# Local attention products of the scan: eight 128x128 block diagonal products in place of 32 of 32x32

## The chip, the cores and the metric

The kernel runs on one core of one Trainium2 chip. The core has a matrix engine (TensorE, in the profile PE for products and PEld for weight loads), VectorE (DVE), ScalarE (ACT), GpSimd (POOL) and SyncE (SP), which issues the DMAs. The metric is the device time of one execution in microseconds.

## What is computed

Two transformer blocks over x of shape (16, 512, 128). The change lies in the second block's attention, a scan over 16 segments of 32 positions, with 16 heads of width 64:

```python
def step(carry, inp):
    mem, z = carry
    q_s, k_s, v_s, qn_s, kn_s = inp
    scores = jnp.einsum('bhnd,bhmd->bhnm', q_s, k_s) * SCALE
    scores = jnp.where(mask, scores, -jnp.inf)
    sdpa = jnp.einsum('bhnm,bhmd->bhnd', jax.nn.softmax(scores, axis=-1), v_s)
    sq = elu1(qn_s)
    num = jnp.einsum('bhnk,bhkv->bhnv', sq, mem)
    den = jnp.einsum('bhnk,bhk->bhn', sq, z)[..., None]
    mem_out = num / (den + 1e-06)
    out = beta * mem_out + (1.0 - beta) * sdpa
    sk = elu1(kn_s)
    prev_v = jnp.einsum('bhnk,bhkv->bhnv', sk, mem) / jnp.einsum('bhnk,bhk->bhn', sk, z)[..., None]
    mem = mem + jnp.einsum('bhnk,bhnv->bhkv', sk, v_s - prev_v)
    z = z + sk.sum(axis=2)
    return ((mem, z), out)
```

The local product is `sdpa`: for each batch and head a 32x32 matrix of exponentials of scores times the 32x64 values; the division by the sums follows in the next stage.

## The kernel before

The program runs stage after stage: weights folded, the first block's projections (`front`), its attention (`attend`), the closing of both (`tail`), routing and experts, and from about 1.68 ms on the scan (`scale_factors`, then `scan`).

The scan handles a pair of heads at a time: 16 segments times 8 pairs are 128 pairs. The 16 batches lie as BG = 4 groups g in the free dimension and B1 = 4 f in the partitions: partitions 32f to 32f+31 hold the 32 positions of batch 4g + f. A tile of a pair therefore has eight "channels" ch = 2g + hh (group and head of the pair) in the free dimension and four f in the partitions.

The order is written by hand: each engine has a loop over steps s, unrolled, and in step s each handles several pairs at different stages. In step s TensorE (the loop at the end of `turn`) does, in this order: query projection of pair s (L2037); local product of pair s-2 (L2071); values of pair s (L2043); key recall of s-2 (L2053 with `sk`); transposes of keys (L2089), mask (L2077) and scores (L2082) of s-1; key projection of s (L2037); query recall of s-2 (L2053 with `sq`); output projection of s-4 (L2101); transpose of heads of s-3 (L2094); memory update of s-4 (L2061). At some steps of each eight, work for the next segment is added (L1883, L1889, L2106, L2176).

VectorE in step s: L2268 scales the local product of s-2 out of PSUM bank 6; rope of the query of s (L2240, L2241) and its feature (L2247); L2278 and L2280 for the key recall; L2285 and L2286 on the scores of s-1; L2297, L2298 and L2300 for the query recall; rope of the key (L2240, L2241); then for pair s-1 the 32x32 transposes of the exponentials `ss` into `pT` (L2306), their sums (L2308) and the reciprocal (L2309); then the memory additions (L2257). Rounding and moments for the next segment stand at some steps between L2286 and L2297 or before.

ScalarE in step s: query features of s (L2186, L2191); copies of the turned keys (L2200) and of the values (L2204); the exponential of the scores of s-1 (L2208); key features (L2186, L2188, L2191); the copy of turned heads (L2220); and at some steps normalization for the next segment (L1863, L1869) and copies of its turned input (L1895, L1899).

Engines wait on named counters (`G[...]`). The local product of pair p waits until `pt` has reached p + 1, and `pt` rises with the reciprocal L2309, so after transpose and sums. The transposed exponentials are the stationary operand, the values the moving one. An f32 product stands in the trace as two weight loads and two matmul records.

Of the kernel before, what the change touches and what calls it, by code (L numbers as in the profile page):

```python
# [25 lines left out]
P = 128  # L26
# [1584 lines left out]
B1, SEG, DH = 4, 32, 64  # L1611
# [3 lines left out]
PAIRS = H // 2  # L1615
# [149 lines left out]
def scan(nc, c, V, out, nseg):  # L1765
# [4 lines left out]
    with ExitStack() as ctx:  # L1770
        sb = lambda n, s, d=F32: ctx.enter_context(nc.sbuf_tensor("sc_" + n, s, d))
        sems = []

        def sem(n):
# [8 lines left out]
        uu = V["uu"]  # L1783
# [8 lines left out]
        GH = 2 * BG  # L1792
        ss, pT = sb("ss", [P, 2, GH, SEG]), sb("pT", [P, 4, GH, SEG])
        mx, sm = sb("mx", [P, GH]), sb("sm", [P, 4, GH])
        rk, rq = sb("rk", [P, GH]), sb("rq", [P, GH])
# [5 lines left out]
        names = ("h_in0 h_in1 stat fact shift_d xn_d tq_d xnn_d xq_d step xt xt_c xqt xqt_c hb_d ffn ffn_c vp v_c pj ex mn rp sn sgq sgk add_d sS skt skc "  # L1801
                 "sx se pt pvd old kr_s qr_s kd ud qd od up mu ott otc oproj yt_c yt ydone stored0 stored1").split()
        G = {n: sem(n) for n in names}
# [3 lines left out]
        def wait(eng, name, n):  # L1807

            if n > 0:
                eng.wait_ge(G[name], n)  # L1810
# [5 lines left out]
        def linker(eng):  # L1816
            count = [0]

            def link(ins):

                count[0] += 1
                ins.then_inc(G["step"], 1)
                eng.wait_ge(G["step"], count[0])
            return link
# [76 lines left out]
        def prepare(seg):  # L1901

            with nc.Block() as block:
# [5 lines left out]
                @block.vector  # L1909
                def _(dve):  # L1910
                    link = linker(dve)
                    moments(dve, link, 0)
                    shifts(dve, 1)
                    round_fp8(dve, link, 1)
# [24 lines left out]
        def turn(seg, more):  # L1939
# [33 lines left out]
            with nc.Block() as block:  # L1973
# [58 lines left out]
                def _(pe):  # L2032
# [33 lines left out]
                    def local(p):  # L2066
                        for g in range(BG):
                            for hh in range(2):
                                for f in range(B1):
                                    ch = 2 * g + hh  # L2070
                                    ins = pe.matmul(ps[32 * f:32 * f + 32, 6, ch * DH:(ch + 1) * DH], pT[32 * f:32 * f + 32, p % 4, ch, :],  # L2071
                                                    uu[32 * f:32 * f + 32, p % PAIRS, g, hh, 0:DH], start=True, stop=True)
                        ins.then_inc(G["pvd"], 1)
# [35 lines left out]
                    for s in range(STEPS):  # L2109
# [5 lines left out]
                        if inside(p):  # L2115
                            wait(pe, "otc", min(s - 3, PT))
                            wait(pe, "pt", p + 1)
                            local(p)
# [61 lines left out]
                def _(act):  # L2180
                    def features(n):
# [9 lines left out]
                        act.activation(ee[:, which], ee[:, which], ACT.Exp, scale=-1.0).then_inc(G["mn"], 1)  # L2191

                    for s in range(STEPS):
                        if s < PT:
                            features(2 * s)
# [36 lines left out]
                def _(dve):  # L2232
# [26 lines left out]
                    for s in range(STEPS):  # L2259
                        p = s - 2  # L2260
                        if inside(p):
                            wait(dve, "pvd", p + 1)
                            wait(dve, "pt", p + 1)
                            wait(dve, "ott", p - 3)
# [39 lines left out]
                        if inside(p):  # L2304
                            wait(dve, "se", p + 1)
                            dve.transpose(pT[:, p % 4].rearrange("p c j -> p (c j)"), ss[:, p % 2].rearrange("p c j -> p (c j)"))  # L2306
                            s_ = sm[:, p % 4]
                            link(dve.tensor_reduce(head(s_), by_head(ss[:, p % 2]), AX.X, ALU.add))  # L2308
                            dve.reciprocal(s_, s_).then_inc(G["pt"], 1)  # L2309
                        if s - 7 in starts:  # L2310
# [155 lines left out]
```

## Time and profile before

| | us |
|---|---|
| median of 3 runs | 3109.3 |
| lowest, highest | 3105.91, 3112.54 |
| profiled execution | 3109.39 |
| span of its trace | 3107.6 |
| TensorE busy, products | 2664.5 (86%) |
| VectorE busy | 2506.4 (81%) |
| ScalarE busy | 1875.9 (60%) |
| GpSimd busy | 1758.7 (57%) |

Busy times are shares of the whole span, and stages differ. A row of a timeline gives the start and the length of a group of equal instructions in us, the engine and the line, what is written and read, the shape and the count; in brackets how long the engine was idle before it and what ended that. "Issue" is idle time in which the engine waited for nothing that the profile shows. Rows of a matmul overlap: the time from one row's start to the next one's is what a stage costs, not its length. The granted clock (PEclk) is 1.00 at 2.4 GHz and 0.50 at 1.2 GHz.

### The profile page before, as it was taken

The numbers are of one execution on the slowest core, as the hardware profiler recorded it, in microseconds if no ns is written. First come the engines' busy times: TensorE is split into PE (matmuls) and PEld (weight loads), VectorE is DVE, ScalarE is ACT, GpSimd is POOL, SyncE is SP. The second block draws the span as 40 slices with busy tenths as digits, with TensorE's granted clock in tenths as the row PEclk, the third lists the DMA queues.
The fourth block names the chain that finished last, engine by engine and source line by source line (L and its number), as shares of the span: only waits on it lengthen the run. The fifth ranks groups of instructions, "written<-read, shape, count | busy, mean of one in ns | idle before, by whom it ended". The sixth has DMA issues, their size and how long they took to land. (4 is left out here: it accounts for less than half of the span.)

```text
span 3107.6 us, 129631 instructions
## 1 busy us (share of the span) xinstructions
PE 2664.5 (86%) x53553; PEld 1513.6 (49%) x53553; DVE 2506.4 (81%) x7598; ACT 1875.9 (60%) x3797; POOL 1758.7 (57%) x1988
## 2 busy tenths in 40 slices
PE   5887999999999999782331899999999998999998
PEld 2442333333333333372220666666666666666665
DVE  4677989999999999586606888888888888888887
ACT  5785999999999999630001555555455555555543
POOL 5883222222222222240063888888888888888886
PEclk9896999999999999895655999999999999999999
DMA  4676434444444443191023000000000000000000
GB/s 126 205 241 155 90 89 94 94 107 94 91 94 98 96 94 87 39 325 55 10 40 91 4 11 11 11 11 4 11 11 11 11 11 11 11 11 5 11 8 11
DMA packets 173633, 201.58 MB, mean 65 GB/s; under 512 B 31152, under 2 KB 134512, under 8 KB 172784
## 3 DMA queue, kind: packets, MB, share of 16 engines
q1 hardware_dynamic: 170480, 191.87, 23.8%
q8 instruction: 427, 7.00, 1.0%
q0 software_dynamic: 2560, 1.35, 0.4%
q14 instruction: 166, 1.36, 0.2%
HBM read 125.10 MB, written 67.24 MB: 62 GB/s over the span
## 5 line engine op out<-in xcount | busy, mean ns | idle before, releaser
L851 ACT ACTIVATE at_pA<-at_ps 128x512 f32<-128x512 f32 x1024 | 551.8, 614 | 57.8 <-DVE at_ps L903 51.1
L912 DVE CUSTOM_DVE_ANT_0 at_junk<-at_ps,w_cmask 128x512 f32<-128x512 f32 (+3 forms) x1024 | 463.4, 485 | 102.7 <-PE at_ps L754 95.4
L903 DVE TENSOR_TENSOR at_ps<-at_ps,w_ratio 128x128 f32<-128x128 f32 (+3 forms) x1024 | 451.2, 491 | 2.1 <-PE at_ps L748 0.5
L720 POOL TENSOR_SCALAR_AFFINE_SELECT at_pB<-at_pB 128x128 f32<-128x128 f32 x256 | 74.8, 292 | 640.4 <-ACT at_pB L857 638.3
L857 ACT ACTIVATE at_pB<-at_ps 128x512 f32<-128x512 f32 (+1 forms) x768 | 379.5, 531 | 53.0 <-PE at_ps L761 47.7
L2001 POOL TENSOR_TENSOR sc_rb<-sc_rb,v_sin 128x512 f32<-128x512 f32 x256 | 326.0, 1274 | 42.4 <-DVE sc_ra L2241 41.1
L2037 PE MATMUL sc_ps<-sc_xT,v_wqkv 128*128 128x512 f32 x512 | 287.2, 644 | 4.0 <-PEq L56 1.4
L748 PE MATMUL at_ps<-at_aq,at_ak 72*128 72x512 bf16 x1024 | 278.3, 388 | 0.2
L2200 ACT COPY sc_skN<-sc_ps 128x512 f32<-128x512 f32 x128 | 75.1, 587 | 324.8 <-PE sc_ps L2089 324.8
L1996 POOL TENSOR_TENSOR sc_sk<-sc_ee,sc_relu 128x512 f32<-128x512 f32 x128 | 165.4, 1293 | 180.8 <-ACT sc_ee L2191 180.7
L761 PE MATMUL at_ps<-at_bq,at_bk 75*128 75x512 bf16 (+3 forms) x1024 | 265.8, 302 | 1.5 <-ACT at_pB L857 0.9
L781 PE MATMUL at_ps<-at_pA,at_v 128*32 128x512 f32 x2048 | 263.0, 609 | 1.2 <-ACT at_oT L840 1.2
L754 PE MATMUL at_ps<-at_bk,at_bq 72*128 72x512 bf16 (+3 forms) x1024 | 225.3, 306 | 20.3 <-PEq L56 11.7
L2186 ACT ACTIVATE sc_ee<-sc_ps 128x512 f32<-128x512 f32 x256 | 150.4, 587 | 110.9 <-PE sc_ps L2037 109.9
L2240 DVE STREAM_SHUFFLE sc_rb<-sc_ps 128x512 f32<-128x512 f32 x256 | 189.4, 740 | 0.0
L2071 PEld LDWEIGHTS sc_ps<-v_uu,sc_pT 32*32 32x32 f32 x8192 | 126.7, 106 | 118.7 <-issue 112.1
L2241 DVE TENSOR_TENSOR sc_ra<-sc_ps,v_cos 128x512 f32<-128x512 f32 x256 | 172.1, 672 | 0.0
L2004 POOL TENSOR_TENSOR sc_kr<-sc_ra,sc_rb 128x512 f32<-128x512 f32 x128 | 163.0, 1273 | 10.0
L2004 POOL TENSOR_TENSOR sc_qr<-sc_ra,sc_rb 128x512 f32<-128x512 f32 x128 | 162.5, 1270 | 10.0
L2257 DVE TENSOR_TENSOR v_mem<-v_mem,sc_ps 128x520 f32<-128x520 f32 x256 | 161.8, 674 | 6.0 <-PE sc_ps L2061 6.0
L2191 ACT ACTIVATE sc_ee<-sc_ee 128x512 f32<-128x512 f32 x256 | 161.4, 631 | 8.2
L2029 POOL TENSOR_TENSOR sc_ol<-sc_ol,sc_t 128x512 f32<-128x512 f32 x128 | 163.1, 1274 | 5.1 <-DVE sc_t L2300 5.1
(317 smaller groups left out, 5949.9 us busy)
## 6 DMA issues: line engine op xcount, KB each, us to landing
parts_scratch<-fr_parts SPq DMA_DIRECT2D x64, 384.0 KB, 4.1
at_bk<-parts_scratch SPq DMA_DIRECT2D x192, 96.0 KB
at_ak<-parts_scratch SPq DMA_DIRECT2D x192, 96.0 KB
v_scratch<-fr_v SPq DMA_DIRECT2D x32, 352.0 KB, 4.4
at_v<-v_scratch SPq DMA_DIRECT2D x32, 352.0 KB, 3.5
at_bq<-parts_scratch SPq DMA_DIRECT2D x128, 64.0 KB
at_aq<-parts_scratch SPq DMA_DIRECT2D x128, 64.0 KB
on_scratch<-at_on SPq DMA_DIRECT2D x32, 256.0 KB, 2.2
```

Of the source, the lines that this page charges most:

```text
L748: pe.matmul(ps[:, BANK[f"A{j}"], :], ak[slot][:, n % 4, j * P:(j + 1) * P], aq[slot][:, n % 4], start=True, stop=True).then_inc(filled, 1)
L754: ins = pe.matmul(ps[:, BANK[kind], col:col + wide], bq[slot][0:ROWS, n % 4, j * P:(j + 1) * P], bk[slot][0:ROWS, n % 4, 0:wide], start=Tr ...
L761: ins = pe.matmul(ps[:, BANK[kind], col:col + S - j * P], bk[slot][:, n % 4, j * P:(j + 1) * P], bq[slot][:, n % 4, j * P:S], start=True, ...
L781: ins = pe.matmul(ps[32 * s:32 * s + 32, PV, q0:S], v[:, b % 2, a, j, h * (HD + 1):h * (HD + 1) + 32], probs, start=(j == 0), stop=(j == N ...
L851: act.activation(pA[:, n % A_RING, j * S:(j + 1) * S], src, ACT.Exp).then_inc(exped, 1)
L857: act.activation(pB[:, n % T_RING, at:at + wide], src[:, 0:wide], ACT.Exp).then_inc(exped, 1)
L903: dve.tensor_tensor(src[:, 0:wide], src[:, 0:wide], W["ratio"][:, S - wide:S], ALU.mult).then_inc(tilted, 1)
L912: ins = dve.tensor_tensor_reduce(junk[:, P * j * (j + 1) // 2:P * (j + 1) * (j + 2) // 2], src[:, col:col + wide], W["cmask"][:, S - wide: ...
L2001: pool.tensor_tensor(by_pos(rb[:, n % 2]), by_pos(rb[:, n % 2]), table("sin", which), ALU.mult).then_inc(G["sn"], 1)
L2004: pool.tensor_tensor(rot[which][:, p % 2], ra[:, n % 2], rb[:, n % 2], ALU.add).then_inc(G["add_d"], 1)
L2037: pe.matmul(ps[:, bank_of("qk"[which], p), :], V["wqkv"][:, col:col + P], xT[:, p // PAIRS % 2], start=True, stop=True).then_inc(G["pj"], 1)
L2240: dve.stream_shuffle(rb[:, n % 2], x, [lane ^ 1 for lane in range(32)])
```

## The change

The local product of a group and a head is made as one 128x128 product. Its stationary operand is a block diagonal matrix: block f of channel ch stands in rows 32f and columns 32f of a new buffer `pB`, which has two sides and is zeroed once before the scan. ScalarE copies the blocks from `pT` into it with four copies (one per f, each 32 partitions, eight channels, 32 columns), at the head of its step. TensorE waits for the new counter `pb` in place of `otc` and `pt`. `pt` now rises with the transpose; VectorE's L2268 waits for the new counter `smd`, which rises with the reciprocal.

```diff
+        pB = sb("pB", [P, 2, GH, B1, SEG])
...
                     link = linker(dve)
+                    dve.memset(pB[:], 0.0)
                     moments(dve, link, 0)
...
                     def local(p):
                         for g in range(BG):
                             for hh in range(2):
-                                for f in range(B1):
-                                    ch = 2 * g + hh
-                                    ins = pe.matmul(ps[32 * f:32 * f + 32, 6, ch * DH:(ch + 1) * DH], pT[32 * f:32 * f + 32, p % 4, ch, :],
-                                                    uu[32 * f:32 * f + 32, p % PAIRS, g, hh, 0:DH], start=True, stop=True)
+                                ch = 2 * g + hh
+                                ins = pe.matmul(ps[:, 6, ch * DH:(ch + 1) * DH], pB[:, p % 2, ch].rearrange("p f j -> p (f j)"),
+                                                uu[:, p % PAIRS, g, hh, 0:DH], start=True, stop=True)
                         ins.then_inc(G["pvd"], 1)
...
                         if inside(p):
-                            wait(pe, "otc", min(s - 3, PT))
-                            wait(pe, "pt", p + 1)
+                            wait(pe, "pb", p + 1)
                             local(p)
...
+                    def place_blocks(p):
+                        wait(act, "pt", p + 1)
+                        wait(act, "pvd", p - 1)
+                        for f in range(B1):
+                            ins = act.copy(pB[32 * f:32 * f + 32, p % 2, :, f], pT[32 * f:32 * f + 32, p % 4])
+                        ins.then_inc(G["pb"], 1)
+
                     for s in range(STEPS):
+                        p = s - 2
+                        if inside(p):
+                            place_blocks(p)
                         if s < PT:
                             features(2 * s)
...
                         if inside(p):
                             wait(dve, "pvd", p + 1)
-                            wait(dve, "pt", p + 1)
+                            wait(dve, "smd", p + 1)
...
                             wait(dve, "se", p + 1)
-                            dve.transpose(pT[:, p % 4].rearrange("p c j -> p (c j)"), ss[:, p % 2].rearrange("p c j -> p (c j)"))
+                            wait(dve, "pb", p - 3)
+                            dve.transpose(pT[:, p % 4].rearrange("p c j -> p (c j)"), ss[:, p % 2].rearrange("p c j -> p (c j)")).then_inc(G["pt"], 1)
                             s_ = sm[:, p % 4]
                             link(dve.tensor_reduce(head(s_), by_head(ss[:, p % 2]), AX.X, ALU.add))
-                            dve.reciprocal(s_, s_).then_inc(G["pt"], 1)
+                            dve.reciprocal(s_, s_).then_inc(G["smd"], 1)
```

ScalarE's queue at the end of one step and the head of the next, in the step that normalizes for the next segment. Before:

```order
L2220 COPY sc_oT<-sc_ps 128x512
L1863 ACTIVATE sc_xn<-sc_ht,sc_shift,sc_sc 128x128 x4
L1869 ACTIVATE sc_tq<-sc_xn,v_qs 128x512
L2186 ACTIVATE sc_ee<-sc_ps 128x512
L2191 ACTIVATE sc_ee<-sc_ee 128x512
L2200 COPY sc_skN<-sc_ps 128x512
```

And after, with the lines of the changed file:

```order
L2230 COPY sc_oT<-sc_ps 128x512
L1864 ACTIVATE sc_xn<-sc_ht,sc_shift,sc_sc 128x128 x4
L1870 ACTIVATE sc_tq<-sc_xn,v_qs 128x512
L2197 COPY sc_pB<-sc_pT 32x8x32 x4
L2186 ACTIVATE sc_ee<-sc_ps 128x512
L2191 ACTIVATE sc_ee<-sc_ee 128x512
L2210 COPY sc_skN<-sc_ps 128x512
```

The four copies stand between the next segment's normalization and the query features.

TensorE's queue around the local product. Before:

```order
L2101 MATMUL sc_ps<-sc_oT,v_wout 128x512
L2094 MATMUL sc_ps<-v_ident,sc_ol 128x128 x4
L2061 MATMUL sc_ps<-v_uu,sc_skN 64x65 x32
L2037 MATMUL sc_ps<-sc_xT,v_wqkv 128x512
L2071 MATMUL sc_ps<-v_uu,sc_pT 32x64 x32
L2043 MATMUL sc_ps<-v_wqkv,sc_xT 128x128 x4
```

And after:

```order
L2102 MATMUL sc_ps<-sc_oT,v_wout 128x512
L2095 MATMUL sc_ps<-v_ident,sc_ol 128x128 x4
L2063 MATMUL sc_ps<-v_uu,sc_skN 64x65 x32
L2039 MATMUL sc_ps<-sc_xT,v_wqkv 128x512
L2072 MATMUL sc_ps<-v_uu,sc_pB 128x64 x8
L2045 MATMUL sc_ps<-v_wqkv,sc_xT 128x128 x4
```

The place is the same; 32 products have become eight.

## Rows read from the trace of the kernel before

**Rows 1.** Busy time and count by engine, clock, DMA; scan's steady part.

```profile
core 0: us, PE busy (x) PEld busy (x) DVE busy (x) ACT busy (x) POOL busy (x), PEclk, DMA share, GB/s
1725.33:3078.69 1353.36, 1253.85 (x43176) 871.27 (x43177) 1160.96 (x2866) 694.34 (x1303) 1127.92 (x905) 0.99 0.04 10
```

**Rows 2.** The line of the local product: durations in ns, first and last start.

```profile
L2071 PE MATMUL sc_ps<-v_uu,sc_pT x8192: 211/214/312, 1714.4 to 3091.0; 32*32 32x64 f32 x200
```

**Rows 3.** Timeline of TensorE's products, one step.

```profile
2506.45 1.10 PE L2071 MATMUL sc_ps<-v_uu,sc_pT 32*32 32x64 f32 x64
2507.49 1.16 PE L2043 MATMUL sc_ps<-v_wqkv,sc_xT 128*128 128x128 f32 x8
...
2512.70 1.12 PE L2101 MATMUL sc_ps<-sc_oT,v_wout 128*128 128x512 f32 x2
2513.66 0.60 PE L2094 MATMUL sc_ps<-v_ident,sc_ol 128*128 128x128 f32 x4
...
2516.20 1.10 PE L2071 MATMUL sc_ps<-v_uu,sc_pT 32*32 32x64 f32 x64
```

**Rows 4.** Timeline of VectorE in the same step.

```profile
2511.53 0.42 DVE L2286 TENSOR_TENSOR sc_ss<-sc_ps,sc_mx 128x256 f32<-128x256 f32 x1
2512.81 0.17 DVE L2297 SCALAR_TENSOR_TENSOR sc_rq<-sc_ps,v_ibeta 128x8 f32<-128x8 f32 x1 [0.86 <-PE sc_ps L2053]
...
2515.09 0.43 DVE L2306 STREAM_TRANSPOSE sc_pT<-sc_ss 128x256 f32<-128x256 f32 x1
...
2515.85 0.20 DVE L2309 RECIPROCAL sc_sm<-sc_sm 128x8 f32<-128x8 f32 x1
```

**Rows 5.** Waits of TensorE in the steady part: us in total, times, longest.

```profile
PE sc_ps L2053 <- issue: 36.9, 62, 1.2
PE sc_ps L2082 <- issue: 19.4, 31, 1.5
PE sc_ps L2061 <- DVE sc_t L2300: 18.5, 19, 3.1
PE sc_ps L2071 <- DVE sc_sm L2309: 6.2, 11, 2.0
```

**Rows 6.** DMA queue of instructions in the steady part: packets, MB, share.

```profile
q8 instruction: 341, 5.59, 1.8%
```

**Rows 7.** Timeline of weight loads and products at L1028, before the scan.

```profile
1336.50 0.97 PEld L1028 LDWEIGHTS tl_ps<-w_wr,tl_xfT 128*128 128x128 f32 x8
1337.39 0.19 PEld L1005 LDWEIGHTS tl_ps<-w_woA,tl_onT 128*128 128x128 f32 x1
...
1336.61 0.96 PE L1028 MATMUL tl_ps<-w_wr,tl_xfT 128*128 128x8 f32 x8
```

**Rows 8.** Timeline of ScalarE in the step of rows 3 and 4.

```profile
2511.99 0.42 ACT L2208 ACTIVATE sc_ss<-sc_ss 128x256 f32<-128x256 f32 x1 [0.85 <-DVE sc_ss L2286]
2512.31 0.58 ACT L2186 ACTIVATE sc_ee<-sc_ps 128x512 f32<-128x512 f32 x1
...
2514.89 1.65 ACT L1863 ACTIVATE sc_xn<-sc_ht,sc_shift,sc_sc 128x128 f32<-128x128 f32 x4
2516.57 0.72 ACT L1869 ACTIVATE sc_tq<-sc_xn,v_qs 128x512 f32<-128x512 f32 x1
```

**Rows 9.** Timelines of two other steps with work for the next segment.

```profile
2347.61 1.65 ACT L1863 ACTIVATE sc_xnn<-sc_ht,sc_shift,sc_sc 128x128 f32<-128x128 f32 x4
...
2347.90 0.44 DVE L2306 STREAM_TRANSPOSE sc_pT<-sc_ss 128x256 f32<-128x256 f32 x1
...
2800.20 0.43 DVE L2306 STREAM_TRANSPOSE sc_pT<-sc_ss 128x256 f32<-128x256 f32 x1
...
2800.65 0.78 ACT L1895 ACTIVATE sc_xT<-sc_ps,v_b,v_g 128x512 f32<-128x512 f32 x1 [1.06 <-PE sc_ps L1883]
```

**Rows 10.** Busy time by engine and clock after a wait of 3.1 us.

```profile
2360.10:2366.00 5.90, 5.88 (x135) 4.09 (x135) 3.20 (x7) 2.00 (x3) 3.77 (x3) 0.50 0.01 3
```

**Rows 11.** Timeline of VectorE where the scan begins.

```profile
1684.33 0.87 DVE L1840 BATCH_NORM_STATS2 sc_st<-sc_ht 128x6 f32<-128x128 f32 x4 [4.41 <-DMA sc_ht<-h_scratch]
```

More of the change, by code:

```diff
@@ L1801, in scan @@
         names = ("h_in0 h_in1 stat fact shift_d xn_d tq_d xnn_d xq_d step xt xt_c xqt xqt_c hb_d ffn ffn_c vp v_c pj ex mn rp sn sgq sgk add_d sS skt skc "
-                 "sx se pt pvd old kr_s qr_s kd ud qd od up mu ott otc oproj yt_c yt ydone stored0 stored1").split()
+                 "sx se pt smd pb pvd old kr_s qr_s kd ud qd od up mu ott otc oproj yt_c yt ydone stored0 stored1").split()
         G = {n: sem(n) for n in names}
```

## Prediction

> **What bounds the kernel now.** The change touches the scan, the last 1.4 ms. I read first the busy time by engine over its steady part [rows 1]: TensorE 1253.85 of 1353.36 us, VectorE 1160.96, ScalarE 694.34, at a granted clock of 0.99. TensorE paces it, VectorE is close behind, ScalarE has room on average. The 8192 records of the local product [rows 2] are 64 for each of 128 pairs (an f32 product stands as two records), from 1714.4 to 3091.0; with about 1.0 us for the last product, that is (3090.1 - 1714.4) / 127 = 10.83 us for one step.
>
> Then one step in order of time. On TensorE [rows 3] the local product starts at 2506.45, the next stage at 2507.49, the query recall is over when L2101 starts at 2512.70, and the next local product starts at 2516.20: a clean step is 9.75 us, so 1.08 us a step is lost on average. On VectorE [rows 4] the chain that starts with the end of the query recall reads: 2512.70 recall over, 2512.81 L2297, 2515.09 transpose (over at 2515.52), 2515.85 the reciprocal L2309 (over at 2516.05), and 0.15 us later the local product starts. So there are two paths from 2512.70 to the next local product, TensorE's own work and VectorE's chain, and they end together: the chain has no slack. That is the place on which all that follows rests.
>
> What is lost besides [rows 5]: "issue" waits of TensorE, 71.3 us over ten rows of that view (the two largest, 36.9 and 19.4, stand in the recalls and the scores, stages of many small records), and waits for VectorE, 18.5 + 6.2. The issue waits look like instruction loading: 341 packets of 16 KB [rows 6] in 1353.36 us are one each 3.97 us, one for 253 of the 86353 records of [rows 1].
>
> **Local product on TensorE.** Removed: 64 records, 2506.45 to 2507.49, 1.04 us [rows 3]. Added: 8 f32 products of 128x128, 16 records, each with a load of 128 columns and only 64 columns to stream. The trace has that shape nearly: L1028 loads 128x128 f32 and streams 8 columns, and its eight loads take 1336.50 to 1337.39, 0.111 us each [rows 7]. With next to nothing to stream this is the price of the load. So 16 x 0.111 = 1.78 us, 0.74 more than before. By columns alone it would be less: L2101's two records of 512 columns take 2512.70 to 2513.66, 0.48 each [rows 3], so 64 columns 0.06 and the product 0.96. I take 1.78, since L1028 is the same load.
>
> The Trainium skill ("TensorE: Matmul & The Clock Gate", LDWEIGHTS) has a load cost its columns over 1.2 GHz whatever the rows. An estimate by that page is 107 ns a load and 1.71 us for the product; L1028's 0.111 agrees.
>
> **Placing on ScalarE.** Four copies 32x256, SBUF to SBUF, stand at the head of ScalarE's step and wait for the transpose; TensorE waits for the last of them. Nearest row: L2208, 128x256 f32 in SBUF, 0.42 us, and the next instruction starts 0.32 after it [rows 8]. 0.04 from VectorE (2511.53 + 0.42 to 2511.99), 3 x 0.32, 0.42: 1.42 us. A quarter of the partitions saves nothing in that reading, as lanes work side by side. Bounds: 0.2 a copy if fewer lanes were cheaper, 0.41 as the four 128x128 of L1863 show (1.65 / 4), which also read a scale and a shift. To TensorE another 0.15 as now, and 0.08 more for the first load, most of the 0.11 from load to product at L1028 (1336.50 to 1336.61).
>
> Moving the signal from the reciprocal to the transpose gives back 2516.05 - 2515.52 = 0.53, which the sum has, as it starts from the transpose. Behind the waiting copies on ScalarE stand the query features (L2186, L2191), which VectorE's next rope waits for; but VectorE stands at the local product itself then (L2268), and the features are over long before that product. So nothing is added there.
>
> **One clean step.** 1.78 (local) + 5.21 (2507.49 to 2512.70) + 0.11 + 2.71 (2512.81 to 2515.52) + 1.42 + 0.23 = 11.46 us, against 9.75. TensorE waits 1.0 us at each local product.
>
> **What comes on top, each step.**
> - ScalarE late: once in eight steps it has L1863 and L1869 for the next segment, until 2517.29, 1.77 after the transpose [rows 8]; a step later another four L1863 until 2349.26 against 2348.34, 0.92; then L1895 until 2801.43 against 2800.63, 0.80 [rows 9]; then a copy of the same kind, some 0.5 (no row, between 0.3 and 0.6). All this stands ahead of the copies and is hidden today. 3.99 / 8 = 0.50.
> - VectorE late (moments and rounding between the scores and L2297): 24.7 us of waits now [rows 5], 0.19 a step; 0.25, as no slack remains beside it.
> - Issue waits inside the part that still counts (all but 2512.70 to 2516.20): 36.9 + 19.4 among them, 0.45 a step. 48 products and 48 loads fewer of some 690 records, and a longer step, let loading keep up better; I take 0.25, bounds 0 and 0.45.
> - Clock: after the longest wait, 3.1 us [rows 5], the granted clock was 0.50 (1.2 GHz instead of 2.4) through 5.90 us [rows 10]. TensorE will now stand 1 us each step and 1.8 to 2.8 us in three of eight. 0.2 a step, bounds 0.1 and 0.5.
>
> Sum 12.66 us, 1.83 more than 10.83; times 127 = 232 us. The zeroing of the block buffer (128x2048 f32 on VectorE) falls into 4.41 us in which VectorE waits for the first load [rows 11]: nothing; at most some 3 us without it. Profiled execution 3109.4 us (span 3107.6), the median of the runs 3109.3; so 3341, I say 3340. With the low ends of all terms (place 1.06, late 0.4 and 0.15, issue 0, clock 0.1) a step is 11.75, 3226; with the high ones (place 1.69, late 0.6 and 0.35, issue 0.45, clock 0.5) 13.63, 3465. All at one end is unlikely: 3240 to 3425.
>
> **Rivals.**
> - Instruction loading decides (faster). If one packet each 3.97 us were a fixed rate and the true bound, a step of some 595 records instead of 691 takes 2.35 packets, 9.3 us, and TensorE's own work 9.75 + 0.74 = 10.49 ends last: 0.34 less, 3066. For it: 71.3 us of issue waits. Against: it holds only if the copies are over before TensorE arrives, thus if the added 0.96 of the chain falls under zero, and [rows 4] shows a chain without slack. 0.04.
> - Placing mostly hidden, TensorE alone pays: 0.74 - 0.25 = 0.49 a step, 3171. It needs copies of about 0.1 us each and ScalarE in time. 0.06.
> - Streaming, not loading, sets the product: 0.96 instead of 1.78, 104 us less than forecast, 3236. L1028 speaks against it, but it streams 8 columns, not 64. 0.06.
> - The clock falls more often: a stretch as that of [rows 10], 5.90 us at half speed, loses some 2.9 us, and with two of them in eight steps (after the two longest waits) the clock costs 0.73 a step, 0.53 beyond my 0.2, 3408. Against: the 3.1 us before it is one of 30 waits for VectorE, and most of those changed nothing. 0.14.
> - The forecast: 0.70.
>
> To the third belongs a sentence of the Trainium skill ("Perfetto Trace Analysis", Matmuls), that larger matmuls are more efficient than smaller ones. By that rule the eight large products should take less than the 1.04 us of the 32, some 0.96; the loads of L1028 speak against it here.
>
> **How the numbers follow.** A measurement of this kernel tells 0.2%, 6 us, from no change. Faster is the first rival, 0.04; within 0.2% is left 0.02 for mixtures of it with the second; slower 0.94. The range 3235 to 3425 holds the forecast and the third and the fourth rival.
>
> **What would show it.** Right: the eight products take 1.7 to 1.9 us with a load each 0.111; ScalarE's four copies take 1.4 us directly after the transpose; TensorE's wait at the local product names ScalarE and is about 1.0 us, some 2.7 in the step with L1863 and L1869; issue waits fall under 45 us; the clock has more low stretches. Wrong: no wait at the local product (placing hidden), 16 records within 1.1 us, copies that take a quarter of L2208's time, or a clock at 0.50 in a large part of the scan.

## The result and the profile after

| | before | after |
|---|---|---|
| median, us | 3109.24 | 3386.35 |
| lowest, highest | 3105.91, 3112.54 | 3374.75, 3388.92 |
| runs | 4 | 4 |
| span of the profiled execution | 3107.6 | 3387.2 |

The ratio of after to before is 1.0883, with a 95% interval of 1.0864 to 1.0902: the change costs 277 us, where the forecast said 231. The time is inside the range of 3235 to 3425.

The page after, the span, the busy shares, the granted clock in 40 slices, and the head of the chain that ended last:

```profile
span 3387.2 us, 117980 instructions
PE 2835.5 (84%) x47409; PEld 1700.3 (50%) x47409; DVE 2501.2 (74%) x7599; ACT 2076.1 (61%) x4309; POOL 1759.0 (52%) x1988
...
PEclk9887999999999998756579998999989999999999
...
PE 30%; DVE 8%; ACT 7%; issue 4%; POOL 0%; DVEq 0%; ACTq 0%
```

TensorE, VectorE and GpSimd all fell in share, and ScalarE did not become full either: the step is longer since the engines wait for each other in turn. Two groups of the page's fifth part (busy us, mean ns | idle us before, and its releaser) name the place, the new products and the new copies:

```profile
L2072 PE MATMUL sc_ps<-v_uu,sc_pB 128*128 128x64 f32 x2048 | 284.2, 297 | 186.3 <-ACT sc_pB L2197 186.3
L2197 ACT COPY sc_pB<-sc_pT 32x256 f32<-32x256 f32 x512 | 205.1, 401 | 59.9 <-DVE sc_pT L2317 55.4
```

The answer to [rows 5]: what TensorE waited for from 1730 to 3355 us (us in total, times, longest).

```profile
PE sc_ps L2072 <- ACT sc_pB L2197: 179.2, 125, 4.1
PE sc_ps L2063 <- DVE sc_t L2310: 19.4, 26, 1.7
PE sc_ps L2055 <- issue: 5.3, 12, 0.6
PE sc_ps L2063 <- issue: 0.2, 1, 0.2
```

The issue waits, 71.3 us before, are 5.5 us. In their place stands a wait for ScalarE's copies at each local product, 179.2 us. VectorE now stands there too, where it waited for the local product 28.9 us in the steady part before. The largest of its waits in the same stretch:

```profile
DVE sc_ol L2278 <- PE sc_ps L2072: 318.4, 125, 6.0
```

The answer to [rows 1], the scan's steady part (columns as there):

```profile
1730.50:3366.50 1636.00, 1428.89 (x37460) 1059.27 (x37460) 1161.56 (x2887) 895.22 (x1814) 1136.47 (x911) 0.92 0.03 8
```

The granted clock has two levels here, 1.00 and 0.50, so a mean of 0.92 is 16% of 1636 us at the low one, some 260; counting the low stretches one by one from 1730 to 3355 us I find 246 us in 55 of them. Before, with a mean of 0.99, it was some 27.

One step, to be laid beside [rows 3]:

```profile
2626.83 2.00 PE L2072 MATMUL sc_ps<-v_uu,sc_pB 128*128 128x64 f32 x16 [1.10 <-ACT sc_pB L2197]
2628.66 1.93 PE L2045 MATMUL sc_ps<-v_wqkv,sc_xT 128*128 128x128 f32 x8
...
2635.11 1.13 PE L2102 MATMUL sc_ps<-sc_oT,v_wout 128*128 128x512 f32 x2
...
2639.66 2.00 PE L2072 MATMUL sc_ps<-v_uu,sc_pB 128*128 128x64 f32 x16 [0.84 <-ACT sc_pB L2197]
```

And the same step on VectorE and on ScalarE, beside [rows 4] and [rows 8]:

```profile
2635.22 0.17 DVE L2307 SCALAR_TENSOR_TENSOR sc_rq<-sc_ps,v_ibeta 128x8 f32<-128x8 f32 x1 [0.96 <-PE sc_ps L2055]
...
2637.49 0.44 DVE L2317 STREAM_TRANSPOSE sc_pT<-sc_ss 128x256 f32<-128x256 f32 x1
```

```profile
2636.71 0.58 ACT L2230 COPY sc_oT<-sc_ps 128x512 f32<-128x512 f32 x1 [0.36 <-PE sc_ps L2095]
2637.96 1.65 ACT L2197 COPY sc_pB<-sc_pT 32x256 f32<-32x256 f32 x4 [0.67 <-DVE sc_pT L2317]
```

This is the chain as it was forecast: the recall is over at 2635.11, the transpose ends at 2637.93, the copies run from 2637.96 to 2639.61, the product starts at 2639.66. It takes 4.55 us, where 0.11 + 2.71 + 1.42 + 0.23 = 4.47 had been forecast.

**The two halves of a step.** For every step of the scan I took the time from the start of the local product to the start of the output projection (L2101 before, L2102 after), called half A, and from there to the next local product, half B. Half A is mostly TensorE's own work. Half B is where VectorE's chain and the copies run. Means over the scan's steps (126 and 125 pairs), in us, with the clock of one stretch, 1740 to 3050 us, beside them:

| kernel | median, us | half A | half B | mean clock |
|---|---|---|---|---|
| before | 3109.24 | 6.95 | 3.87 | 0.99 |
| forecast | 3340 | 7.44 | 5.22 | |
| after | 3386.35 | 7.75 | 5.18 | 0.92 |
| e1_no_copies | 3090.97 | 6.93 | 3.68 | 1.00 |
| e2_small_products | 3233.04 | 6.53 | 5.18 | 0.99 |
| e3_signal_only | 3094.36 | 6.91 | 3.85 | 0.99 |
| e4_copies_first | 3279.32 | 7.25 | 4.82 | 0.97 |
| e5_transpose_first | 3300.67 | 7.56 | 4.76 | 0.94 |
| e6_both_early | 3159.03 | 7.03 | 4.09 | 1.00 |
| e7_before_transpose_first | 3096.73 | 6.74 | 3.98 | 0.99 |
| e8_wait_filled | 3320.69 | 7.23 | 5.24 | 0.98 |
| e9_full_copies (one run) | 3308.65 | 7.43 | 4.89 | 0.95 |
| e10_flat_copies (one run) | 3309.76 | 7.41 | 4.92 | 0.96 |

The forecast's row is its sum put into the same halves: A = 1.78 + 5.21 + 0.25 (issue) + 0.20 (clock), B = 4.47 + 0.50 + 0.25 (ScalarE and VectorE late). Half B came out at 5.18 against 5.22. Half A is 0.31 us longer than forecast, and that times 127 is 39 of the 46 us that the forecast lacked. The experiments look for what stands in it.

### The profile page after: what moved, and what is told of

The parts are those of the page before. It is cut to its first block and busy times, and to the rows that moved or that the text cites. A ratio compares the mean times of both kernels' runs of the same rounds, so it can differ in the third digit from the quotient of the medians.

```text
span 3387.2 us, 117980 instructions
## 1 busy us (share of the span) xinstructions
PE 2835.5 (84%) x47409; PEld 1700.3 (50%) x47409; DVE 2501.2 (74%) x7599; ACT 2076.1 (61%) x4309; POOL 1759.0 (52%) x1988
## 5 line engine op out<-in xcount | busy, mean ns | idle before, releaser
L2072 PE MATMUL sc_ps<-v_uu,sc_pB 128*128 128x64 f32 x2048 | 284.2, 297 | 186.3 <-ACT sc_pB L2197 186.3
L2072 PEld LDWEIGHTS sc_ps<-v_uu,sc_pB 128*128 128x128 f32 x2048 | 264.6, 209 | 290.6 <-ACT sc_pB L2197 290.6
L2278 DVE SCALAR_TENSOR_TENSOR sc_ol<-sc_ps,v_rest,sc_sm 128x256 f32<-128x256 f32 x256 | 112.1, 480 | 327.0 <-PE sc_ps L2072 327.0
L2197 ACT COPY sc_pB<-sc_pT 32x256 f32<-32x256 f32 x512 | 205.1, 401 | 59.9 <-DVE sc_pT L2317 55.4
L2045 PE MATMUL sc_ps<-v_wqkv,sc_xT 128*128 128x128 f32 x1024 | 190.0, 345 | 1.7 <-DVE sc_ra L2251 1.7
L2250 DVE STREAM_SHUFFLE sc_rb<-sc_ps 128x512 f32<-128x512 f32 x256 | 188.4, 736 | 0.0
L2251 DVE TENSOR_TENSOR sc_ra<-sc_ps,v_cos 128x512 f32<-128x512 f32 x256 | 172.5, 674 | 0.0
L2045 PEld LDWEIGHTS sc_ps<-v_wqkv,sc_xT 128*128 128x128 f32 x1024 | 168.6, 249 | 3.5 <-DVE sc_ra L2251 2.5
L748 PEld LDWEIGHTS at_ps<-at_aq,at_ak 72*128 72x128 bf16 x1024 | 88.5, 97 | 158.6 <-DVE at_mx L912 75.3
```

What stands on the lines that cost most here:

```text
L748: pe.matmul(ps[:, BANK[f"A{j}"], :], ak[slot][:, n % 4, j * P:(j + 1) * P], aq[slot][:, n % 4], start=True, stop=True).then_inc(filled, 1)
L2045: ins = pe.matmul(ps[:, bank_of("v", p), g * P:(g + 1) * P], xT[:, p // PAIRS % 2, g * P:(g + 1) * P], V["wqkv"][:, col:col + P], start=Tr ...
L2072: ins = pe.matmul(ps[:, 6, ch * DH:(ch + 1) * DH], pB[:, p % 2, ch].rearrange("p f j -> p (f j)"), uu[:, p % PAIRS, g, hh, 0:DH], start=Tr ...
L2197: ins = act.copy(pB[32 * f:32 * f + 32, p % 2, :, f], pT[32 * f:32 * f + 32, p % 4])
```

## The experiments

The first four ran beside a run of before with a median of 3112.41 us, the next four beside one of 3116.65, the last two beside one of 3103.03. Ratios are to the before of the same chip. Differences between medians of different groups mix chips: the gains of 107, 86, 227 and 66 us over the changed kernel that are given below come out as 108, 92, 232 and 71 by the ratios. The mean clock of a row is that of its profiled execution.

### The large products without the copies

From the changed kernel:

```diff
-                            wait(pe, "pb", p + 1)
+                            wait(pe, "otc", min(s - 3, PT))
+                            wait(pe, "pt", p + 1)
                             local(p)
...
-                        p = s - 2
-                        if inside(p):
-                            place_blocks(p)
...
-                            wait(dve, "pb", p - 3)
+                            wait(dve, "pvd", p - 3)
```

> Changed kernel (3386 us) without the four copies; TensorE waits for the transpose itself. The block buffer stays zero, so the local attention part of the output is left out; all products run. Theory (the wait for ScalarE and the low clock that follows it are most of the 277 us; the eight products alone cost 0.79 us a step, given back in part as issue waits vanish): 3120 to 3165 us, wait at the local product near 0, low clock under 40 us of the scan. Rival (the eight products with 16 full weight loads are the main cost): above 3250 us.

Measured: 3090.97 us, ratio 0.9937 (0.9920 to 0.9953). It is below both what my theory and what its rival gave; of the theory, the vanished wait and a low clock under 40 us (some 9 us here) came true. Without the copies the eight large products do not cost the scan anything. The stretch from 1740 to 3050 us, the waits of TensorE from 1730 to 3050, and a step of TensorE:

```profile
1740.00:3050.00 1310.00, 1273.18 (x36660) 960.71 (x36660) 1139.11 (x2828) 684.53 (x1284) 1115.57 (x892) 1.00 0.04 10
```

```profile
PE sc_ps L2063 <- DVE sc_t L2308: 26.6, 24, 1.7
PE sc_ps L2055 <- issue: 8.5, 24, 0.6
```

```profile
2500.53 1.12 PE L2102 MATMUL sc_ps<-sc_oT,v_wout 128*128 128x512 f32 x2
...
2503.83 1.89 PE L2072 MATMUL sc_ps<-v_uu,sc_pB 128*128 128x64 f32 x16
2505.56 1.11 PE L2045 MATMUL sc_ps<-v_wqkv,sc_xT 128*128 128x128 f32 x8
```

The packets of its instruction queue from 1740 to 3050 us, beside [rows 6]:

```profile
q8 instruction: 291, 4.77, 1.5%
```

The product is no cheaper than forecast: 2503.83 to 2505.56 is 1.73 us, 0.69 more than the 32 small ones of [rows 3]. But TensorE is busy for 1273 of 1310 us, and its issue waits have shrunk from 71.3 us to 9.4, some 0.5 us a step. With a few smaller terms that pays for the 0.69: half A is 6.93 us against 6.95. That the issue waits are instruction loading is still a reading; it fits that the packets now come 4.50 us apart instead of 3.97 and 2.36 to a step, where the first rival had 2.35. Without the copies nothing of the loss is left. This doesn't make the products free in the changed kernel, as the next run shows. In this run the block buffer holds zeros; the kernel with both moves below has real blocks, hardly any wait, and the same clock of 1.00.

### The copies with the small products

From the changed kernel; the copies are still made and still waited for, though nothing reads them. VectorE's transpose also waits for `pvd`, which keeps it from overwriting what the small products read:

```diff
-                                ch = 2 * g + hh
-                                ins = pe.matmul(ps[:, 6, ch * DH:(ch + 1) * DH], pB[:, p % 2, ch].rearrange("p f j -> p (f j)"),
-                                                uu[:, p % PAIRS, g, hh, 0:DH], start=True, stop=True)
+                                for f in range(B1):
+                                    ch = 2 * g + hh
+                                    ins = pe.matmul(ps[32 * f:32 * f + 32, 6, ch * DH:(ch + 1) * DH], pT[32 * f:32 * f + 32, p % 4, ch, :],
+                                                    uu[32 * f:32 * f + 32, p % PAIRS, g, hh, 0:DH], start=True, stop=True)
```

> Changed kernel with the four copies and the wait for them kept, but the local product made as before, 32 products of 32x32 out of the transposed tile. Theory (chain plus clock cost most, products 0.79 us a step, and the issue waits come back by 0.2 to 0.4 us a step): 3386 - 100 + 35 = 3320 us, 3290 to 3350. Rival (products are the main cost): under 3250 us.

Measured: 3233.04 us, ratio 1.0397 (1.0377 to 1.0418). It fell on the side of the rival: my theory had left the low clock where it was, and it went with the large products. The same stretch, and TensorE's waits from 1730 to 3055:

```profile
1740.00:3050.00 1310.00, 1113.95 (x38441) 778.35 (x38444) 1030.61 (x2574) 796.93 (x1616) 1012.07 (x808) 0.99 0.04 9
```

```profile
PE sc_ps L2073 <- ACT sc_pB L2198: 161.0, 112, 4.0
PE sc_ps L2055 <- issue: 10.1, 20, 1.2
```

Half B is 5.18 us, the same as in the changed kernel: it does not depend on the form of the products. Half A is 6.53, shorter than before the change (6.95): in the longer step the issue waits are down to 17 us here too. From this kernel to the changed one half A grows by 1.22 us a step, 155 us in 127 steps, and the medians differ by 153. Of the 1.22, the product at the full clock is 0.79 (1.83, from 2626.83 to 2628.66 above, less 1.04). The rest, 0.43, goes with the clock: 0.99 here and 0.92 there. So a wait of 1.4 us a step alone hardly brings the low clock (this kernel), and the large products alone don't either (the one before this). Together they do. The waits one by one say it more sharply: of those from 1.05 to 1.6 us, all 88 in this kernel passed without a low stretch, and 38 of 91 in the changed one were followed by one; of the longer waits it is 11 of 18 here and 17 of 17 there.

In us over the before of the same chip, the large products without copies are 21 less, the copies with small products 121 more, and both 277 more. So the copies alone are less than half of the loss. The rest comes only when copies and large products meet: the product's 0.79 us, for which a step that waits for the copies has hardly any issue waits left to give back, and the clock.

### The moved signal alone

From the kernel before:

```diff
-                            wait(dve, "pt", p + 1)
+                            wait(dve, "smd", p + 1)
...
-                            dve.transpose(pT[:, p % 4].rearrange("p c j -> p (c j)"), ss[:, p % 2].rearrange("p c j -> p (c j)"))
+                            dve.transpose(pT[:, p % 4].rearrange("p c j -> p (c j)"), ss[:, p % 2].rearrange("p c j -> p (c j)")).then_inc(G["pt"], 1)
...
-                            dve.reciprocal(s_, s_).then_inc(G["pt"], 1)
+                            dve.reciprocal(s_, s_).then_inc(G["smd"], 1)
```

> Kernel before with one part of the change alone: the counter the local product waits for rises with the transpose, the reciprocal has its own. Theory (the chain recall, VectorE, local product had no slack, and the signal comes 0.53 us earlier; TensorE alone needs 3.50 of the 3.91 us it takes now): 0.2 to 0.4 us a step, 3060 to 3085 us. Rival (TensorE and instruction loading set the step, not the chain): 3103 to 3115 us, no change.

Measured: 3094.36 us, ratio 0.9941 (0.9924 to 0.9957): a gain, between what theory and rival gave. TensorE's waits from 1740 to 3050:

```profile
PE sc_ps L2053 <- issue: 30.3, 55, 1.3
PE sc_ps L2061 <- DVE sc_t L2300: 22.5, 19, 2.8
PE sc_ps L2082 <- issue: 20.9, 31, 1.5
```

The wait at L2071 for the reciprocal, 6.2 us in [rows 5], is no longer among the larger ones. The issue waits are all but unchanged: 66.3 us over all rows of this 1310 us stretch, against 71.3 in 1353. So a chain 0.53 us shorter is worth some 18 us of the 67 that 127 such steps would give: TensorE's own queue ends at the same time. With the kernel of the earlier transpose below, from which it can't be told apart, it is the fastest version with the whole local product, and its edit is part of the change.

### The copies before the next segment's normalization

From the changed kernel, the call moved on ScalarE:

```diff
-                        p = s - 2
-                        if inside(p):
-                            place_blocks(p)
                         if s < PT:
...
                             act.copy(oT[:, p % 2], ps[:, 6, :]).then_inc(G["otc"], 1)
+                        p = s - 1
+                        if inside(p):
+                            place_blocks(p)
                         for j in at_step(s, 3):
```

> Changed kernel with the four copies moved ahead of ScalarE's normalization and input copies for the next segment, otherwise the same. Theory (those stand ahead of the copies in four of eight steps and make them up to 1.8 us late, 0.5 us a step, and the longest waits also bring most of the low clock): 3386 - 63 - 20 = 3300 us, 3280 to 3325, low clock clearly less than 246 us. Rival (the lateness is hidden elsewhere): above 3360 us.

Measured: 3279.32 us, ratio 1.0535 (1.0512 to 1.0558), 107 us below the changed kernel. Half B fell by 0.36 us, half A by 0.50. The wait at the local product from 1730 to 3055:

```profile
PE sc_ps L2072 <- ACT sc_pB L2197: 111.0, 108, 3.4
```

The term "ScalarE late" was 0.50 a step; half B gives 0.36. The larger part of this gain stands in half A, in which TensorE has the same instructions in the same order. Waits over 1.6 us are down from 17 to 3, and low stretches from 55 to some 24; the mean clock is 0.97 instead of 0.92.

### The transpose before the turned heads

From the changed kernel, VectorE's transpose moved ahead of the second rope of the step:

```diff
-                        if s < PT:
-                            rope(2 * s + 1)
                         p = s - 1
...
                             dve.transpose(pT[:, p % 4].rearrange("p c j -> p (c j)"), ss[:, p % 2].rearrange("p c j -> p (c j)")).then_inc(G["pt"], 1)
+                        if s < PT:
+                            rope(2 * s + 1)
+                        p = s - 1
+                        if inside(p):
                             s_ = sm[:, p % 4]
```

> Changed kernel with VectorE's transpose ahead of the key's rope (1.24 us earlier in its queue). Theory (the chain query recall, VectorE, four copies, local product sets the step, and its waits bring the low clock): the wait at the local product falls by up to 1.2 us a step, the low clock under 100 us, 3150 to 3200 us. Rival (TensorE's own longer product sets the step): above 3300 us.

Measured: 3300.67 us, ratio 1.0586 (1.0552 to 1.0620). The expectation missed by 100 us, and the low clock was some 200 us instead of under 100. By its time the rival (above 3300) holds, but not by its mechanism: TensorE still waited 101.2 us for the copies from 1730 to 3140. ScalarE's waits for the transpose from 1730 to 3140 us, and two neighbouring groups on ScalarE:

```profile
ACT sc_pB L2197 <- DVE sc_pT L2315: 2.1, 11, 0.4
```

```profile
2507.04 0.59 ACT L2230 COPY sc_oT<-sc_ps 128x512 f32<-128x512 f32 x1
2507.53 1.64 ACT L2197 COPY sc_pB<-sc_pT 32x256 f32<-32x256 f32 x4
```

The copies hardly ever wait for the transpose now. They stand behind ScalarE's own queue: its key features, the copy of the turned heads (L2230), which in 56 of 113 steps also waits for products that TensorE makes after the recall (25.2 us), and the next segment's work. I had counted only the chain that I shortened. Half B fell by 0.42 of the 1.22 us that the rope takes (2636.27 to 2637.49, L2250 and L2251, in the changed kernel).

### Both moves together

From the kernel of the earlier copies, with the same move of the transpose:

```diff
-                        if s < PT:
-                            rope(2 * s + 1)
...
                             dve.transpose(pT[:, p % 4].rearrange("p c j -> p (c j)"), ss[:, p % 2].rearrange("p c j -> p (c j)")).then_inc(G["pt"], 1)
+                        if s < PT:
+                            rope(2 * s + 1)
```

> The edits of the two kernels with the earlier transpose and with the copies ahead of the next segment's work together. Theory: the copies end before TensorE arrives in nearly all steps, so the time comes near that without copies (3091 us): 3095 to 3130 us. Rival (ScalarE's 1.64 us a step cost time wherever they stand): above 3180 us.

Measured: 3159.03 us, ratio 1.0137 (1.0106 to 1.0168), between my range and the rival's. TensorE's waits from 1730 to 3140 us, a step of TensorE, and the same on ScalarE:

```profile
PE sc_ps L2072 <- ACT sc_pB L2197: 25.4, 54, 2.2
```

```profile
2604.76 1.13 PE L2102 MATMUL sc_ps<-sc_oT,v_wout 128*128 128x512 f32 x2
...
2608.54 2.00 PE L2072 MATMUL sc_ps<-v_uu,sc_pB 128*128 128x64 f32 x16 [0.31 <-ACT sc_pB L2197]
```

```profile
2605.69 0.63 ACT L2191 ACTIVATE sc_ee<-sc_ee 128x512 f32<-128x512 f32 x1
2606.36 0.59 ACT L2227 COPY sc_oT<-sc_ps 128x512 f32<-128x512 f32 x1
2606.85 1.64 ACT L2197 COPY sc_pB<-sc_pT 32x256 f32<-32x256 f32 x4
```

Against the kernel without copies half B is still 0.41 us longer and half A 0.10: 65 us in 127 steps, and the medians differ by 68. In the step shown what is left is ScalarE's own queue: the key features (L2191), L2227, four copies, each directly behind the one before, and the product 0.05 us after the last. In other steps L2227 waits for TensorE's L2095 (41 of 126, 21.3 us) or the copies for the transpose (26, 19.6 us). TensorE's waits for the copies, 25.4 us, are 0.20 a step, half of what half B is longer. The moves together gain 227 us over the changed kernel, where one alone gains 107 and the other 86. That is 34 us more than the sum of the two.

The move of the transpose was put into the kernel before as well, with the moved signal; the edit without what it takes out further down.

```diff
+                        p = s - 1
+                        if inside(p):
+                            wait(dve, "se", p + 1)
+                            dve.transpose(pT[:, p % 4].rearrange("p c j -> p (c j)"), ss[:, p % 2].rearrange("p c j -> p (c j)")).then_inc(G["pt"], 1)
                         if s < PT:
```

> Kernel before with the signal on the transpose and the transpose ahead of the key's rope. Theory (with the signal alone, 3094 us, the wait at the local product is gone already, and issue waits are what is left): 3088 to 3100 us, within 0.2% of that. Rival (the chain still costs in the steps with rounding and moments): 3060 to 3085 us.

Measured: 3096.73 us, ratio 0.9937 (0.9918 to 0.9957), as the moved signal alone and as expected. The earlier transpose helped only where the copies hang on it.

### The wait filled with work

From the changed kernel, a product of 128x128 by 128x512 whose result is overwritten, ahead of the wait:

```diff
                         if inside(p):
+                            wait(pe, "otc", min(s - 3, PT))
+                            pe.matmul(ps[:, 6, :], V["wqkv"][:, 0:P], V["wqkv"][:, 0:S], start=True, stop=True)
                             wait(pe, "pb", p + 1)
```

> Changed kernel with one more f32 product of 128x512, 1.06 us of TensorE work whose result is overwritten, ahead of the wait at the local product. Theory (the low clock, 246 us of the scan, comes from TensorE standing still there and costs some 0.8 us a step): low clock under 80 us, 3290 to 3345 us although work is added. Rival (the clock costs little, or falls because of the loads of the eight products): low clock over 180 us, 3385 to 3420 us.

Measured: 3320.69 us, ratio 1.0656 (1.0622 to 1.0689). With a microsecond of needless work added to each step the kernel is 66 us faster. The stretch, and the wait from 1730 to 3140:

```profile
1740.00:3050.00 1310.00, 1216.87 (x31207) 862.78 (x31207) 968.76 (x2411) 750.30 (x1521) 952.12 (x759) 0.98 0.03 8
```

```profile
PE sc_ps L2072 <- ACT sc_pB L2199: 62.6, 95, 2.7
```

Half B is 5.24 against 5.18: the copies end when they did. Half A is 7.23 against 7.75, with the same instructions in it; 0.52 x 127 = 66 us, the whole gain. The low clock fell from some 246 us to some 81, at the edge of what theory gave. Waits of 1.05 to 1.6 us no longer occur in it. This is the cleanest sight of what the clock costs.

### The partitions of a copy

From the changed kernel, each of the four copies over all 128 partitions, first with the same strides:

```diff
-                            ins = act.copy(pB[32 * f:32 * f + 32, p % 2, :, f], pT[32 * f:32 * f + 32, p % 4])
+                            ins = act.copy(pB[:, p % 2, :, f], pT[:, p % 4])
```

and then with both sides contiguous:

```diff
+                            ins = act.copy(flat(pB[:, p % 2, 2 * f:2 * f + 2].rearrange("p c f j -> p (c f) j")), flat(pT[:, p % 4]))
```

> Changed kernel whose four copies each cover all 128 partitions (the same 256 elements a partition, same strides), so every block is written over all rows and the local product is not the reference's. In the changed kernel the copies start 0.41 us apart and do not overlap, against 0.32 for the nearest row. Theory (each of them starts on another 32 partitions, and that is what keeps them apart): with all partitions 0.32 apart, four in 1.38 us. Rival (the copy itself costs 0.41, by its strides or as copy, whatever the partitions): 1.63 us again.

> The same with both sides contiguous: four copies of 128 partitions by 256 contiguous elements, the block places not respected, so the local product is not the reference's. Theory (partitions decide): as with full partitions, 1.38 us for four. Rival (the strides of 32 elements out of 128 on the writing side decide): 1.63 us with strides, 1.38 us here.

Measured: 3308.65 and 3309.76 us, one run each, 1.066 and 1.067 times the one run of before on that chip. Four copies on ScalarE, of the first and of the second:

```profile
2602.95 1.32 ACT L2197 COPY sc_pB<-sc_pT 128x256 f32<-128x256 f32 x4 [0.67 <-DVE sc_pT L2317]
```

```profile
2602.75 1.32 ACT L2197 COPY sc_pB<-sc_pT 128x256 f32<-128x256 f32 x4 [0.67 <-DVE sc_pT L2317]
```

Theory held against its rival both times. Four copies of 128 partitions take 1.32 us, four of 32 partitions 1.65: (1.32 - 0.40) / 3 = 0.31 us from one start to the next against (1.65 - 0.40) / 3 = 0.41. The narrow copies move a quarter of the data, and four of them take longer, though one is as long as a wide one (0.401 us in the mean): they don't overlap. Strides made no difference. Whether it is the count of partitions or the changing first partition that takes the overlap away was not told apart.

## Why the prediction was right, and where it was off

- **The place.** Right. The chain through VectorE had no slack, the copies came on top of it, and TensorE's wait at the local product names ScalarE, 179.2 us or 1.43 a step, against 1.0 + 0.50 forecast. In the step with L1864 and L1870 it was to be some 2.7; the trace has 2.94:

```profile
2582.07 1.65 ACT L1864 ACTIVATE sc_xn<-sc_ht,sc_shift,sc_sc 128x128 f32<-128x128 f32 x4
2583.76 0.72 ACT L1870 ACTIVATE sc_tq<-sc_xn,v_qs 128x512 f32<-128x512 f32 x1
2584.38 1.63 ACT L2197 COPY sc_pB<-sc_pT 32x256 f32<-32x256 f32 x4
```

```profile
2586.07 2.13 PE L2072 MATMUL sc_ps<-v_uu,sc_pB 128*128 128x64 f32 x16 [2.94 <-ACT sc_pB L2197]
2587.99 2.02 PE L2045 MATMUL sc_ps<-v_wqkv,sc_xT 128*128 128x128 f32 x8
```

- **Local product.** 1.78 forecast, 1.83 measured at the full clock, 1.73 where no wait stands ahead of it; with the low clock in it the mean over the steps from 1740 to 3050 is 2.03. The loads of [rows 7] held: 16 loads in 1.86 us, from the first to L2045's first (2628.61) 1.78, 0.111 each. The third rival, 0.96, is out.

```profile
2626.83 1.86 PEld L2072 LDWEIGHTS sc_ps<-v_uu,sc_pB 128*128 128x128 f32 x16 [1.92 <-ACT sc_pB L2197]
```

- **Copies.** 1.42 forecast with the 0.04 ahead of them, 1.64 measured for the four as a mean over the steps, beyond 1.42 but within the 0.41 a copy of the bounds. The row taken, L2208, has 128 partitions and overlaps with its neighbour. The 0.23 from the copies to the product was 0.05 in the step shown, so that the two errors nearly cancel: 4.55 against 4.47.
- **ScalarE late, VectorE late.** 0.50 and 0.25 forecast. Moving the copies ahead of the next segment's work gave 0.36 in half B; the waits for VectorE are 19.4 / 127 = 0.15. Half B as a whole, 5.18 against 5.22, leaves little error.
- **Issue waits.** 0.25 forecast, 5.5 / 127 = 0.04 measured. What was left came near the lower bound, 0: more was given back than forecast. Both the longer step and the fewer records do it: the copies with small products have 17 us, the large products without copies 9.4.
- **Clock.** This is the term that was mis-sized, beyond its bounds: 0.20 forecast, with bounds of 0.1 and 0.5, some 0.7 measured. Half A after, 7.75, less half A without copies, 6.93, is 0.82. Of that 0.10 is the product's first load, which stands behind the wait now (1.83 against 1.73; without copies it started 0.30 us ahead of the product, at 2503.53). Some 0.7 is left for the clock, and the filled wait got 0.52 of it back. The 0.43 between small and large products above is less, since the small ones with their wait have some low clock and issue waits too. A clock at 0.50 in a large part of the scan was named as a sign of being wrong; it was 15% of it. The fourth rival, 0.73 and 3408 us, had the right size; it put it into two stretches in eight steps, and there are 55 stretches in 127 steps, of some 4.5 us each. Taken with the forecast's terms that were too large (issue by 0.21, VectorE late by 0.10), its sum overshot by 22 us, and the forecast's fell short by 46. That the time still lies well inside the range owes something to luck: the clock was too small by 0.5, and issue and VectorE too large by 0.31.
- **Where the low clock begins.** What I did not foresee is that a wait of 1.05 to 1.6 us can be enough here: 38 of the 55 low stretches follow one, the other 17 a wait over 1.6 us. Of the 55, 30 begin in the local product, 17 in the products after it and 8 in the wait. A step of TensorE, and the clock (last but two of the columns) in slices of a microsecond:

```profile
2599.80 2.20 PE L2072 MATMUL sc_ps<-v_uu,sc_pB 128*128 128x64 f32 x16 [1.46 <-ACT sc_pB L2197]
2601.79 2.02 PE L2045 MATMUL sc_ps<-v_wqkv,sc_xT 128*128 128x128 f32 x8
```

```profile
2600.00:2601.00 1.00, 1.00 (x11) 1.00 (x10) 0.00 (x0) 0.97 (x2) 1.00 (x2) 1.00 0.58 137
2601.00:2602.00 1.00, 1.00 (x9) 1.00 (x8) 0.00 (x0) 0.03 (x1) 0.86 (x1) 0.72 0.44 103
2602.00:2603.00 1.00, 1.00 (x7) 1.00 (x7) 0.96 (x4) 0.00 (x0) 0.00 (x0) 0.50 0.55 149
...
2605.00:2606.00 1.00, 1.00 (x57) 0.88 (x58) 0.88 (x2) 0.44 (x1) 0.92 (x2) 1.00 0.00 0
```

  Here the clock falls near the end of the local product, and L2045 takes 1.95 us to the next row's start where it takes some 1.04 at the full clock. In the forecast a wait was weighed by its length alone, by the 30 waits for VectorE before. But those stood ahead of the small products of L2061 and L2071, and these ahead of sixteen records that load 128 columns and stream 64.
- **Zeroing the block buffer.** Nothing, as forecast. It takes 1.76 us on VectorE and fits into the wait for the first load; from the last instruction before it to L1841 it is 1682.87 to 1687.48, 4.61 us, against 1679.63 to 1684.33, 4.70, before. The scan starts some 3 us later after the change, through earlier stages that the change doesn't touch.
- **First rival, instruction loading.** Out as a result, but not as a mechanism. Where nothing waits for copies, the issue waits did give back most of what the large products cost. The forecast's 0.04 rested on the copies being hidden, and they were not.

Added up, a step grew by 7.75 + 5.18 - 6.95 - 3.87 = 2.11 us in the means of the halves. From the first and last local product it is (3369.1 - 1.8 - 1718.7) / 127 = 12.98 us against 10.83, 2.15 more, 273 us. Forecast were 1.83 and 232. The record gives the lower end of the range once as 3240 and once as 3235; the time is inside either.

The Trainium skill ("Perfetto Trace Analysis", Matmuls) prefers larger matmuls to smaller ones. By TensorE's time for the product alone this case goes against it: 1.83 or 1.73 us for eight against 1.04 for 32. By the kernel's time without the copies it is even: 3090.97 against 3094.36 for the small ones with the same signal, ratios 0.9937 (0.9920 to 0.9953) and 0.9941 (0.9924 to 0.9957).

What stays open: why a wait of 1.05 to 1.6 us brings the low clock with the large products behind it and not with the small ones, and why after 38 of 91 and not after all. The runs show that wait or products alone leave the mean at 0.99 or 1.00, and that both give 0.92; nothing here tells the mechanism.

## What to carry to other kernels

When a matmul is rebuilt into fewer and larger ones, cost it by its loads if it streams fewer columns than it loads (f32 with 8 and with 64 columns here), and then ask who makes the new operand and on whose chain that stands: here the large products were free alone, 1.6 us of copies on a chain without slack cost 4% with the small products, and both together cost 9%. Before a path is shortened, write down the path that ends next on every engine that takes part; two moves that gave 107 and 86 us alone gave 227 together. A TensorE wait that stands in each step can cost more than its length: look at the granted clock right behind it.

## What the hardware did that I had not expected

- Four ScalarE copies of 32 partitions, each at another first partition, take 1.65 us, and four of 128 partitions with the same 256 columns 1.32. The narrow ones start 0.41 us apart, the wide ones 0.31.
- After 38 of 91 waits of 1.05 to 1.6 us ahead of eight products of 128x128 by 64 columns the clock fell to 0.50, and after none of 88 such waits ahead of 32 products of 32x32 by 64. With the 17 after longer waits that is 55 stretches of together some 246 us. A needless product of about 1 us in the wait cut that to some 81 us and the kernel by 66 us.
- Issue waits of TensorE fell from 71.3 us to 9.4 with 48 products and 48 loads fewer a step, and to 17 us with all the records in place and a longer step.
